# Two attention layers on one core: output weights split earlier in a unit, the first softmax between the leading queries

## The reference

```python
# layer 0: 16 heads of 96, 4 key heads, keys = context and tokens
s = jnp.concatenate([context, latents], axis=1)
q = (latents @ Wq.T); k = (s @ Wk.T); v = (s @ Wv.T)
out = softmax(q @ k.T / sqrt(96)) @ v
x = x + tanh(g) * (out @ Wo.T)
# layer 1: 32 heads of 128, 8 key heads, keys = context, q and k rms-normalised
q = rmsnorm(x @ Wq.T, q_norm_w); k = rmsnorm(ctx @ Wk.T, k_norm_w)
out = softmax(q @ k.T / sqrt(128) + mask) @ v
x = x + tanh(g) * (out @ Wo.T)
```

## Time and profile before

| | |
|---|---|
| median of 3 runs | 2771.48 us (2769.73 to 2779.86) |
| the profiled execution | 2768.73 us |
| its span, first to last instruction | 2766.9 us |
| PE busy | 2489.0 us, 90% |
| DVE, ACT, POOL busy | 1335.7, 1018.3, 714.3 us |
| mean granted clock of PE | 0.940 |
| attention of layer 0 | about 849 to 1360 us of the span |
| attention of layer 1 | about 1594 to 2574 us |

### The profile page before, as it was taken

The page is one execution under the profiler, slowest core; times in us unless marked ns, Lnnn a source line. Parts: engine busy times, 40 slices in busy tenths (PEclk is TensorE's granted clock), DMA queues, the critical chain, the costliest instruction groups (busy, mean ns, idle before and its releaser), DMA issues. The chain is left out here.

```text
span 2766.9 us, 33590 instructions
## 1 busy us (share of the span) xinstructions
PE 2489.0 (90%) x12768; PEld 2191.2 (79%) x12768; DVE 1335.7 (48%) x2137; ACT 1018.3 (37%) x2306; POOL 714.3 (26%) x608
## 2 busy tenths in 40 slices
PE   8999999799996899998869689999999999997834
PEld 6888888589996688886659577999999999986823
DVE  6222222133103465665353446666666666655697
ACT  3222222123212555555210235544555455553323
POOL 3000000000003233332021054545554555542020
PEclk9999999899997899999889889999999999999657
DMA  6222221253232123222021032333333323322001
GB/s 198 69 69 69 69 69 58 73 173 99 77 92 86 51 85 88 85 70 56 17 69 39 17 87 75 102 104 103 91 97 104 103 91 96 103 91 64 6 0 48
DMA packets 159361, 217.46 MB, mean 79 GB/s; under 512 B 31510, under 2 KB 124082, under 8 KB 158178
## 3 DMA queue, kind: packets, MB, share of 16 engines
q1 hardware_dynamic: 159202, 215.33, 25.6%
HBM read 176.99 MB, written 38.29 MB: 78 GB/s over the span
## 5 line engine op out<-in xcount | busy, mean ns | idle before, releaser
L1053 POOL TENSOR_TENSOR attend_w_hi<-attend_w_raw,attend_one 128x1024 fp32r<-128x1024 f32 (+1 forms) x184 | 334.0, 1830 | 141.0 <-PE attend_ps_gemm L1338 85.2
L1338 PE MATMUL attend_ps_gemm<-normed_hi,attend_w_hi 128*128 128x400 f32 x704 | 267.6, 380 | 37.6 <-DVE attend_w_lo L1206 37.6
L1338 PE MATMUL attend_ps_gemm<-attend_o_hi,attend_w_hi 128*128 128x400 f32 x704 | 259.0, 368 | 44.7 <-DVE attend_w_lo L1206 36.9
L1206 DVE TENSOR_TENSOR attend_w_lo<-attend_w_raw,attend_w_hi 128x1024 fp32r<-128x1024 f32 (+1 forms) x184 | 215.2, 1202 | 152.9 <-POOL attend_w_hi L1053 151.8
L1117 ACT ACTIVATE attend_p<-attend_p,attend_neg_max 100x361 f32<-100x361 f32 x256 | 150.7, 590 | 271.7 <-DVE attend_neg_max L1245 271.7
L1338 PE MATMUL attend_ps_gemm<-attend_o_hi,attend_w_lo 128*128 128x400 f32 x704 | 249.3, 354 | 0.0
L1338 PE MATMUL attend_ps_gemm<-attend_o_lo,attend_w_hi 128*128 128x400 f32 x704 | 249.2, 354 | 0.0
L1338 PE MATMUL attend_ps_gemm<-normed_lo,attend_w_hi 128*128 128x400 f32 x704 | 244.0, 347 | 0.0
L1338 PE MATMUL attend_ps_gemm<-normed_hi,attend_w_lo 128*128 128x400 f32 x704 | 242.8, 345 | 0.0
L1417 PE MATMUL attend_ps_out<-attend_pt,attend_v_in 121*128 121x400 f32 (+4 forms) x640 | 239.8, 514 | 0.0
L1271 DVE SCALAR_TENSOR_TENSOR stream_tokens<-attend_ps_gemm,attend_gate,stream_tokens 128x400 f32<-128x400 f32 x192 | 121.3, 633 | 203.1 <-PE attend_ps_gemm L1338 201.9
(11 more groups left out here) (262 smaller groups left out, 5708.4 us busy)
## 6 DMA issues: line engine op xcount, KB each, us to landing
attend_w_raw<-in_wq SPq DMA_DIRECT2D x88, 512.0 KB, 4.4
attend_w_raw<-in_wo SPq DMA_DIRECT2D x64, 512.0 KB, 3.7
attend_w_raw<-in_wo SPq DMA_DIRECT2D x32, 384.0 KB, 4.0
context_ctx_raw<-in_ctxT SPq DMA_DIRECT2D x8, 1456.0 KB, 7.1
attend_k_raw<-scratch_k SPq DMA_DIRECT2D x64, 180.5 KB, 5.3
context_ctx_raw<-in_ctxF SPq DMA_DIRECT2D x22, 512.0 KB
scratch_v<-context_v_out SPq DMA_DIRECT2D x44, 256.0 KB, 2.2
scratch_k<-context_kt_out SPq DMA_DIRECT2D x44, 256.0 KB, 5.0
```

What stands on the lines that cost most here:

```text
L1053: pool.tensor_tensor(hi, w_flat(w_raw, j % RAW, j), one[:hi.shape[0]].to_broadcast(hi.shape), ALU.mult).then_inc(w_hi_done, 1)
L1206: dve.tensor_tensor(w_flat(w_lo, j % SPLIT, j), w_flat(w_raw, j % RAW, j), w_flat(w_hi, j % SPLIT, j).bitcast(F32), ALU.subtract).then_inc ...
L1338: mm = pe.matmul(out, left[a](c), right[b](c), start=(c == 0 and a == b == 0), stop=(c == chunks - 1 and a == 1))
```

## The change

Nothing is computed otherwise; only the places in the engines' lists move.

- **Early output splits.** DVE splits the output tile of unit `u + 1` right behind the maxima of pair 0 in unit `u`, ahead of the first `accumulate`; only the query tile's split stays at the end of the unit. POOL rounds that output tile first in the unit, ahead of the key split. In the last unit three of the last four output tiles are split at that early place, and the fourth behind the first two of the final eight accumulates.
- **The start.** The score pairs (0, 0), (0, 1) and (1, 0) follow the last three leading queries one by one; ACT's exponentials and DVE's maxima are put between the queries' copies and remainders in the same way. POOL splits the keys of units 0 and 1 earlier, and SP loads the keys of unit 2 ahead of the last leading tile.
- **Layer 1** computes eight leading queries in place of seven; unit 0 has none.

```diff
--- before.py
+++ after.py
@@ -832,7 +832,7 @@
     QT = HG * HD // P
     REST = P - HD
     NQ = 2 * G * QT
-    LEAD = 2 * QT - (layer == 1)
+    LEAD = 2 * QT
     Q_COPIES = O_COPIES = 1
     if layer == 0:
         Q_COPIES, O_COPIES = 2, 1 + QT
@@ -914,7 +914,7 @@
         def query_of(u):
 
             if layer == 1:
-                n = u + LEAD
+                n = u + LEAD - 1 if u else NQ
             elif u % HB == 0:
                 return None
             else:
@@ -958,10 +958,16 @@
         def w_flat(w, slot, j):
             return w[:, slot] if tiles[j][0] == "q" else w[:, slot, 0:QT * (D // HB)]
 
+        def output_tiles(u):
+            if u == NU:
+                return [place["o", v] for v in range(NU - HB, NU)]
+            return [place["o", u - HB]] if HB <= u < NU else []
+
+        def query_tiles(u):
+            return [place["q", query_of(u)]] if u < NU and query_of(u) is not None else []
+
         def step_tiles(u):
-
-            return [place[t] for t in (("o", u - HB), ("q", query_of(u))) if t in place] if u < NU else \
-                [place["o", v] for v in range(NU - HB, NU)] if u == NU else []
+            return output_tiles(u) + query_tiles(u)
 
         @block.sync
         def _(sp):
@@ -1011,11 +1017,12 @@
                 keys(u)
             for u in range(V_SLOTS - 1):
                 values(u)
-            for j in range(RAW, LEAD):
-                tile(j)
-            for j in step_tiles(0) + step_tiles(1):
+            for j in range(RAW, LEAD - 1):
                 tile(j)
             keys(K_SLOTS)
+            tile(LEAD - 1)
+            for j in step_tiles(1):
+                tile(j)
             for u in range(NU):
                 keys(u + K_SLOTS + 1)
                 values(u + V_SLOTS - 1)
@@ -1082,16 +1089,17 @@
                 weights(j)
                 if j >= SPLIT - 1:
                     squares(j - SPLIT + 1)
-            split_keys(0)
+                if j == LEAD - 3:
+                    split_keys(0)
+            split_keys(1)
             for n in range(LEAD - SPLIT + 1, LEAD):
                 squares(n)
-            split_keys(1)
-            for j in step_tiles(0):
-                weights(j)
             split_keys(2)
             for u in range(NU):
+                for j in output_tiles(u + 1):
+                    weights(j)
                 split_keys(u + 3)
-                for j in step_tiles(u + 1):
+                for j in query_tiles(u + 1):
                     weights(j)
                 squares(query_of(u))
 
@@ -1170,8 +1178,10 @@
                 if layer == 1 and n == HG:
                     copy_sums(0)
                     roots(0)
-            exps(0, 0)
-            exps(0, 1)
+                if n == LEAD - 3:
+                    exps(0, 0)
+                if n == LEAD - 2:
+                    exps(0, 1)
             exps(1, 0)
             normalise(0)
             exps(1, 1)
@@ -1276,14 +1286,13 @@
             for j in range(SPLIT, LEAD):
                 remainder_q(j - SPLIT)
                 split(j)
-            for n in range(LEAD - SPLIT, LEAD):
-                remainder_q(n)
+            remainder_q(LEAD - 3)
             if layer == 1:
                 scales(0)
-            for j in step_tiles(0):
-                split(j)
             maxima(0, 0)
+            remainder_q(LEAD - 2)
             maxima(0, 1)
+            remainder_q(LEAD - 1)
             maxima(1, 0)
             invert(0)
             maxima(1, 1)
@@ -1292,6 +1301,8 @@
                 copy_turn(u, 1)
                 invert(u + 1)
                 maxima(u + 2, 0)
+                for j in output_tiles(u + 1)[:SPLIT]:
+                    split(j)
                 if u >= HB:
                     accumulate(u - HB, 0)
                 if NCH == 4:
@@ -1311,12 +1322,15 @@
                                           ).then_inc(o_lo_done, 1)
                 if layer == 1 and k == 1 and u + HB < NU:
                     scales(i + 1)
-                for j in step_tiles(u + 1):
+                for j in query_tiles(u + 1):
                     split(j)
                 remainder_q(query_of(u))
             for u in range(NU - HB, NU):
                 for half in range(2):
                     accumulate(u, half)
+                for j in output_tiles(NU)[SPLIT:]:
+                    if u == NU - HB:
+                        split(j)
 
         @block.tensor
         def _(pe):
@@ -1424,10 +1438,8 @@
                     turn_sums(0)
                 if layer == 1 and n:
                     sum_squares(n - 1)
-                if n == LEAD - 2:
-                    scores(0, 0)
-            scores(0, 1)
-            scores(1, 0)
+                if n >= LEAD - 3:
+                    scores((n - LEAD + 3) // 2, (n - LEAD + 3) % 2)
             scores(1, 1)
             for u in range(NU):
                 i, k = u // HB, u % HB
@@ -1437,7 +1449,7 @@
                 if u >= HB:
                     outputs(u - HB, 0)
                 if layer == 1:
-                    sum_squares(u + LEAD - 1)
+                    sum_squares(u + LEAD - 2 if u else NU)
                 turns(u, 2)
                 if NCH == 4:
                     turns(u, 3)
```

## The result

**2705.8 us** (median of 4 runs, 2702.36 to 2708.94) against 2770.68 us of the kernel before (4 runs, 2769.73 to 2779.86): ratio 0.9762, 95% interval 0.975 to 0.9774. The forecast was 2709.0 us, in a range of 2692 to 2736. The profiled execution took 2702.36 us, 66.4 us less than the one before; it is the fastest of its four, so that its terms add up to 1.5 us more than the medians show (64.9).

What follows compares the result with a forecast made beforehand. PE bounds nearly all of layer 1; elsewhere it idles at low clock, mostly waiting for DVE's split `attend_w_lo`. Gains at the splits and both starts sum to 62.5 us, giving a median of 2709 us, range 2692 to 2736.

Steps and rivals of the forecast that it cites:

- units 5, 9, 13, 17, 21 of layer 0: Units behind queryless ones in layer 0: the early split brings them to their busy 14.62 us, gain 11.3 us.
- units 25 to 29: Layer 0: 64.41 us at clock 0.92 fall to 50.4 with 0.6 left for a late `o_lo`, gain 13.4 us.
- units 30, 31: Layer 0's end, to the first of the last four outputs: 29.48 us less 8.1 and 13.1, gain 8.3 us.
- units 62, 63: Layer 1's end: 22.08 us now; unit 62 becomes 7.9, unit 63 worsens from 11.9 to 12.6, gain 1.6 us.
- start of layer 0: Leading queries between score pairs cover the first two waits; the fourth pair starts 7.4 us earlier, gain 7 us.
- start of layer 1: Maxima no longer wait behind the eighth tile's split (5.7 us); gain between 0 and 11 us, taken as 6.
- middle of layer 1: Up to unit 56 a query already hides the split: gain 0, and no cost, as POOL and DVE have idle time.
- The new wait: Layer 0's unit 31: third split waits for POOL's rounding, copy for `weigh_values` queued behind it; 13.1 us to `o_lo`.
- Last outputs of both layers: Final outputs of each layer lose their idle time: 3.4 us in layer 0, 4.3 us in layer 1.
- the first rival: The clock does not recover, as low clock comes from other idle time: gain 47.5 us, 2724 us; chance 0.15.
- the rival's place: Layer 1, units 4 to 56: DVE becomes the bound, losing to POOL; 2735 us, or 2785 or more; chance 0.07.
- The next waits: Queryless units: pair 1's scores wait for pair 0's exponentials, 0.5 us margin; 2736 us; chance 0.08.

Runs made afterwards that it cites:

- experiment 1: The change's two halves, each alone against the kernel before: early rounding and splits with the old start, 2717.84 us; the new start with late splits, 2762.34 us.
- experiment 4: Changed kernel with GpSimd's old order (key split first, then both roundings), VectorE's split still early: 2884.8 us; follow-ups 2846.99 (split behind accumulates), 2709.66 us (keys issued ahead).
- e4_where_due: Changed kernel with the early rounding and split only in units without a query of their own, the old place elsewhere: 2706.39 us.
- experiment 3: Changed kernel with extra VectorE reductions behind the early split in units 3 to 55 of layer 1: two more 2706.68 us, four more 2820.1 us.

## Why the prediction was right, step by step

The sum of the terms was 62.5 us; the two profiled executions differ by 66.4 us. The mechanisms held, but the nearness of the sum is in part luck: six terms came out 8.5 us above their forecast together, the other four that missed it 4.6 us below.

| term | forecast us | measured us |
|---|---|---|
| units 5, 9, 13, 17, 21 of layer 0 | 11.3 | 9.4 |
| units 25 to 29 | 13.4 | 13.1 |
| units 30, 31 | 8.3 | 8.3 |
| layer 0's last outputs | 3.4 | 6.2 |
| units 58 to 61 of layer 1 | 7.2 | 7.8 |
| units 62, 63 | 1.6 | 3.0 |
| layer 1's last outputs | 4.3 | 6.2 |
| start of layer 0 | 7 | 8.5 |
| start of layer 1 | 6 | 6.3 |
| middle of layer 1 | 0 | -0.1 |
| all else | 0 | -2.3 |

- **Early split in layer 0.** The mechanism held, and experiment 1 shows it without the new start. The five units behind queryless ones went to 15.05 us and not to 14.62: I cut the idle time to nothing, but the first transposition into a bank freed by VectorE's copy, queued behind `o_lo`, still waits 0.4 us (five of the 7 times above that make 2.9 us). That wait was named for unit 30 and forgotten for these. In units 25 to 29 TensorE's only idle time is 0.6 us ahead of unit 28's first output, where `o_lo` was forecast to be late by as much (the trace names no releaser there); the unit takes 10.96 us.
- **Unit 31.** The new wait came as worked out: the third split sits idle for GpSimd, with the copy behind it. TensorE waits 1.67 us for that copy; 21.2 us to the first output were forecast and measured. VectorE in unit 31, then TensorE:

```profile
1293.86 0.96 DVE L1216 TENSOR_TENSOR attend_w_lo<-attend_w_raw,attend_w_hi 128x768 fp32r<-128x768 f32 x1 [2.05 <-POOL attend_w_hi L1060]
...
1295.28 0.57 DVE L1273 COPY attend_pt<-attend_ps_turn 100x400 f32<-100x400 f32 x1
```

```profile
1295.90 0.91 PE L1431 MATMUL attend_ps_out<-attend_pt,attend_v_in 100*96 100x400 f32 x2 [1.67 <-DVE attend_pt L1273]
1299.53 0.42 PE L1352 MATMUL attend_ps_gemm<-attend_o_hi,attend_w_hi 128*128 128x400 f32 x1 [2.72 <-issue]
```

- **Last outputs of both layers.** The terms were mis-sized: I took only the idle time and left the low clock (0.77 and 0.87). With no idle time inside them they ran at 0.89 and 0.91, 2.8 and 1.9 us better than forecast. So a stretch without idle time can be slow, behind a unit with some; the argument against the first rival, that none in its tables was, doesn't hold in general. Layer 0's took 15.0 to 16.3 us in the runs whose work there is the same, so the 6.2 us of the table are good to about 1 us.
- **Units 62 and 63.** 19.1 us, forecast 20.5. The clean end units were 9.63 us and not 9.9, and unit 63 11.4 and not 12.6: a wait of 3.5 us for `o_lo` behind the third split, the forecast wait at a smaller size.
- **Middle of layer 1.** Cost 0, by the cover that was named: GpSimd's idle time and 2.7 us before the query's bank. The contention of the earlier trace rows appears in 51 of these 53 units. The Trainium skill, "SBUF — State Buffer" (section "SBUF: two separate sides"), has the loser blocked for the whole instruction, and the traces agree: `k_lo` 1.84 us for 0.98, and in experiment 4 a split 2.90 us for 1.22 beside a rounding. It cost nothing, as e4_where_due shows, because it stayed inside the slack that experiment 3 measures. What I had not priced is how near the other order lay: the rival's place was right (VectorE queued behind GpSimd), but GpSimd's new order, which rounds ahead of the keys and which I costed only as a part of the move, decides: without it the kernel takes 179 us more, 114 more than the kernel before.
- **Starts.** The fourth pair of scores came 34.8 us after the first leading matmul (forecast 35, before 42.4). Layer 1's start gave 6.0 to 6.5 us in the ten runs that have it and no further edit there. That it met the forecast of 6 is luck: 6 was a choice between 0 and 11. Of the two waits named, the one of 7.7 us is down to 1.7 at most, and the one on the sums in unit 1 stayed, 4.2 us for 3.6. Layer 0's start depends on where the low clock falls: to unit 5 it took 107.1 to 107.4 us in three profiled executions and 109.2 to 110.3 in nine others with the same start, against 115.7 and 114.7 with the old one. The 8.5 us of the table are of the better kind; in the other nine the start gave 5.4 to 6.5 us, and the forecast of 7 lies between.
- **The rivals.** The clock did recover where the stalls went. The next waits were the ones named, 0.4 to 0.6 us in a unit, but for the last units. The 1.9 us that the stage behind layer 1's attention got longer, at a clock of 0.70 instead of 0.72 in its last 69 us, need no cause in the change: in the twelve experiments, which leave that stage as it is, it took 191.1 to 195.1 us (192.6 before, 194.5 after).
